# Self-loops under a sort key of their own, added as a scale per node, and hop loops of 102 written-out groups

## What is computed

```python
src = concatenate([s, d, arange(6250)]); dst = concatenate([d, s, arange(6250)])   # then sorted by dst

def spmm(edge_row, edge_col, edge_val, dense):
    msgs = edge_val[:, None] * dense[edge_col]
    return segment_sum(msgs, edge_row, num_segments=6250)

h = maximum(layernorm(x), 0)
support = h @ weight
h1 = spmm(src, dst, edge_weight, support)
h2 = spmm(src, dst, edge_weight, h1)
x = x + relu(hop_w[0] * h1 + hop_w[1] * h2 + h)
h = maximum(layernorm(x), 0)
agg = segment_sum(h[src], dst, num_segments=6250)
h = (1.0 + eps) * h + agg
h = elu(bn(h @ W1 + b1)); h = elu(bn(h @ W2 + b2)); h = elu(bn(h @ W3 + b3))
x = x + h @ W4 + b4
```

## Time and profile before

| what | us |
| --- | --- |
| median of 3 runs | 4452.27 (4449.58 to 4452.95) |
| the profiled execution | 4446.35 |
| its span, first to last instruction | 4444.7 |
| before hop 1's first gather | 452.3 |
| hop 1 | 1109.0 |
| hop 2 and the turn to the third gather | 1118.0 |
| third gather stage | 1060.7 |
| dense layers | 705 |

### The profile page before, as it was taken

The page is one execution under the profiler, slowest core; times in us unless marked ns, Lnnn a source line. Parts: engine busy times, 40 slices in busy tenths (PEclk is TensorE's granted clock), DMA queues, the critical chain, the costliest instruction groups (busy, mean ns, idle before and its releaser), DMA issues. The chain is left out here.

```text
span 4444.7 us, 50645 instructions
## 1 busy us (share of the span) xinstructions
PE 3284.7 (74%) x15959; PEld 2715.9 (61%) x15959; DVE 1873.4 (42%) x4492; ACT 797.2 (18%) x1969; POOL 2662.6 (60%) x2708
## 2 busy tenths in 40 slices
PE   6698677777777767777777774566666665998998
PEld 5297555555555555656555654555555555887887
DVE  7898333333333233333333332222222224556766
ACT  4098000000000000000000000000000001545656
POOL 1077677777777677777777766777777775001000
PEclk9899999999999999999999996788888887999999
DMA  4000333333333433333333344433333332223323
GB/s 142 1 5 13 96 108 113 110 109 109 114 109 108 101 104 109 109 114 109 109 108 112 109 99 134 125 105 105 104 105 104 105 105 87 98 89 134 95 65 116
DMA packets 205564, 443.83 MB, mean 100 GB/s; under 512 B 47053, under 2 KB 121089, under 8 KB 205289
## 3 DMA queue, kind: packets, MB, share of 16 engines
q0 software_dynamic: 126464, 336.63, 26.2%
q1 hardware_dynamic: 78933, 105.26, 7.2%
HBM read 382.22 MB, written 59.49 MB: 99 GB/s over the span
## 5 line engine op out<-in xcount | busy, mean ns | idle before, releaser
L1885 PE MATMUL ps<-work 128*128 128x256 f32 x6912 | 1615.3, 387 | 591.2 <-DMA work<-table_hop,idx 591.2
L792 POOL DMA_INDIRECT work<-table_hop,idx x1728 | 1660.2, 961 | 555.7 <-issue 522.1
L1885 PEld LDWEIGHTS ps<-work 128*128 128x128 f32 x6912 | 1288.5, 191 | 916.2 <-DMA work<-table_hop,idx 493.3
L837 POOL DMA_INDIRECT work<-table_gin,idx x832 | 791.0, 951 | 281.7 <-issue 229.5
L1960 PE MATMUL ps<-work 128*128 128x128 f32 x3328 | 571.8, 343 | 411.2 <-DMA work<-table_gin,idx 382.2
L1960 PEld LDWEIGHTS ps<-work 128*128 128x128 f32 x3328 | 526.1, 249 | 481.1 <-DMA work<-table_gin,idx 324.7
L1423 DVE TENSOR_SCALAR work<-iota,w_hi,edge_buf 128x256 f32<-128x256 bf16 x1728 | 583.4, 409 | 17.9 <-issue 16.6
L948 ACT COPY idx<-w 128x8 int32 (+1 forms) x216 | 42.3, 197 | 1951.7 <-PE ps L1885 1950.9
L1536 DVE TENSOR_TENSOR sum_b<-sum_b,ps 128x256 f32 x104 | 43.9, 422 | 799.2 <-PE ps L1960 799.2
L1435 DVE TENSOR_TENSOR sum_b<-sum_b,ps 128x512 f32 x108 | 74.2, 688 | 720.2 <-PE ps L1885 720.2
L1435 DVE TENSOR_TENSOR big<-big,ps 128x512 f32 x108 | 74.3, 688 | 694.2 <-PE ps L1885 694.2
(11 more groups left out here) (225 smaller groups left out, 2609.3 us busy)
## 6 DMA issues: line engine op xcount, KB each, us to landing
work<-table_hop,idx POOLq DMA_INDIRECT x1728, 2.7
z_dram<-sum_b SPq DMA_DIRECT2D x24, 964.0 KB, 4.1
sum_b<-z_dram SPq DMA_DIRECT2D x24, 964.0 KB, 5.2
work<-table_gin,idx POOLq DMA_INDIRECT x832, 2.7
big<-x SPq DMA_DIRECT2D x12, 512.0 KB, 6.0
table_hop<-work SPq DMA_DIRECT2D x12, 512.0 KB, 2.9
table_hop<-sum_b SPq DMA_DIRECT2D x12, 512.0 KB, 3.2
x_dram<-big SPq DMA_DIRECT2D x12, 512.0 KB, 3.5
```

Source lines behind the costliest of these rows:

```text
L792: pool.indirect_dma_start(hop_rows[:, par, t, :], None, table[n], bass.IndirectOffsetOnAxis(idx[:, k % HR, t:t + 1], 0)).then_inc(rows_in[ ...
L837: pool.indirect_dma_start(rows[:, par, t, :], None, table[2], bass.IndirectOffsetOnAxis(idx[:, q, t:t + 1], 0)).then_inc(rows_in[par][half ...
L1885: mm = pe.matmul(ps[:, HWIN * par + b, 0:D], hot[:, par, t, b * P:(b + 1) * P], hop_rows[:, par, t, :], start=(t == 0), stop=(t == GT - 1))
```

## The change

A loop gets the key 49, behind the windows (`NK` = 50 keys), so that the windows' edges fill 102 groups and the loops seven more behind them (`LGROUPS`), which no hop gathers. In the first eight groups of hop 1 DVE builds one-hots of the loops' nodes and PE sums the loop weight of each node with them (`loop_sum`). In hop 1 SP reads `support` back, chunk by chunk, and DVE adds it times `loop_sum` to the sums; hop 2's share of the loops is `loop_scale` on h1 in place of the constant of `keep_h1`. All 102 groups of both hops are written out. `make_bins` now works on bf16 pairs in two halves. Some semaphores are merged.

```diff
+NK = NT + 1
-HBODY = 18
-HITER = 6
-HGROUPS = HBODY * HITER
+HGROUPS = 102
+LGROUPS = 7
+TGROUPS = HGROUPS + LGROUPS
...
+PACE = 8.5
...
 def over_hop(eng, step):
 
-    for k in range(HBODY):
-        step(0, k, True, False)
-    with eng.Fori(1, HITER - 1) as i:
-        for k in range(HBODY):
-            step(i, k, False, False)
-    for k in range(HBODY):
-        step(HITER - 1, k, False, True)
+    for k in range(HGROUPS):
+        step(k)
...
+def chunk_at(k, at):
 
+    for c in range(FULL - 1):
+        if k == at + int(PACE * (c + 1)):
+            return c, c % 2
     return None, None
```

On SP's queue, in hop 1:

```diff
+            def support_load(c):
+                if c > 0:
+                    sp.wait_ge(loop_added, c)
+                sp.dma_start(support_in, rows_of(table[0], c, CT - 1)).then_inc(support_back, 16)
+                sp.dma_start(support_in3, table[0][c * CN + (CT - 1) * P:(c + 1) * CN, :]).then_inc(support_back, 16)
+
+            def hop1_step(k):
+                if k == GT:
+                    sp.wait_ge(loop_mm, GT)
+                    sp.dma_start(support_tail, table[0][FULL * CN:ROWS, :]).then_inc(support_back, 16)
+                    support_load(0)
+                c, q = chunk_at(k, 2)
                 if c is not None:
-                    sp.wait_ge(hop_add, HBODY * i + k + 1)
+                    support_load(c + 1)
+                    sp.wait_ge(hop_add, k + 1)
                     h1_out(c, CT)
```

On DVE, the keys and their one-hots at the start:

```diff
-            dve.wait_ge(edges_in, 64)
-            dve.tensor_copy(dst_all, dst_i).then_inc(dst_cast, 1)
+            dve.wait_ge(edges_in, 96)
+            dve.tensor_copy(dst_all, dst_i)
             dve.tensor_copy(src_all, src_i)
             chain(dve.tensor_scalar(ints, src_i, 7, 127, ALU.logical_shift_right, ALU.bitwise_and))
-            chain(dve.tensor_copy(bin_of, ints))
+            chain(dve.tensor_copy(packed, ints))
+            dve.tensor_tensor(ints.bitcast(F32), src_all, dst_all, ALU.is_equal).then_inc(dst_cast, 1)
+            dve.wait_ge(dst_cast, 1)
+            at_ = [P, TILES, 2]
+            chain(dve.scalar_tensor_tensor(out=bin_twice, in0=ints.bitcast(F32).unsqueeze(2).to_broadcast(at_), scalar=float(NT),
+                                           in1=packed.unsqueeze(2).to_broadcast(at_), op0=ALU.mult, op1=ALU.max))
...
             def make_bins(t):
 
-                windows = iota[:, 0:NT].unsqueeze(1).to_broadcast([P, BINS, NT])
-                of = bin_by_step[:, t, :].unsqueeze(2).to_broadcast([P, BINS, NT])
-                dve.tensor_tensor(bins_of_all(t), windows, of, ALU.is_equal).then_inc(bins_made, 1)
+                at_ = [P, HB, NK // 2, 2]
+                keys = iota[:, 0:NK].rearrange("p (a u) -> p a u", u=2).unsqueeze(1).to_broadcast(at_)
+                for half in range(2):
+                    of = bin_by_step[:, t, half * HB:(half + 1) * HB, :].unsqueeze(2).to_broadcast(at_)
+                    last = dve.tensor_tensor(bins_of(t, half).rearrange("p (g a u) -> p g a u", g=HB, u=2), keys, of, ALU.is_equal)
+                last.then_inc(bins_made, 1)
```

On DVE, in hop 1 (LSTEP is 7):

```diff
+            def loop_hots(k):
+                if k > 0:
+                    dve.wait_ge(loop_mm, k)
+                for u in range(LSTEP):
+                    n = LSTEP * k + u
+                    dve.tensor_scalar(loop_lo_hot[u], iota[:, 0:P], loop_lo[:, n:n + 1], w_sorted[:, HTILES + n:HTILES + n + 1],
+                                      ALU.is_equal, ALU.mult)
+                at_ = [P, LSTEP, NT]
+                dve.tensor_tensor(loop_hi_hot, iota[:, 0:NT].unsqueeze(1).to_broadcast(at_),
+                                  loop_hi[:, LSTEP * k:LSTEP * (k + 1)].unsqueeze(2).to_broadcast(at_),
+                                  ALU.is_equal).then_inc(loop_hot, 1)
...
+            def add_loops(c, tiles):
+                dve.wait_ge(support_back, 16 * (1 + 2 * min(c + 1, FULL)))
+                for t in range(tiles):
+                    of = support_tail if c == FULL else support_in3 if t == CT - 1 else support_in[:, t, :]
+                    b = CT * c + t
+                    to = hop1_sum[:, b * D:(b + 1) * D]
+                    last = dve.scalar_tensor_tensor(out=to, in0=of, scalar=loop_sum[:, b:b + 1], in1=to, op0=ALU.mult, op1=ALU.add)
+                last.then_inc(loop_added, 1)
...
+            def keep_h1_and_loops(c, tiles):
+                for t in range(tiles):
+                    b = CT * c + t
+                    to = base[:, b * D:(b + 1) * D]
+                    last = dve.scalar_tensor_tensor(out=to, in0=hop1_sum[:, b * D:(b + 1) * D], scalar=loop_scale[:, b:b + 1], in1=to,
+                                                    op0=ALU.mult, op1=ALU.add)
+                last.then_inc(h1_kept, 1)
...
+            def hop1_step(k):
+                group(0, k, hop1_sum)
+                if k < GT:
+                    loop_hots(k)
+                if k == GT:
+                    loop_scales()
+                c, q = chunk_at(k, 1)
                 if c is not None:
...
+                    add_loops(c, CT)
```

On PE, in hop 1:

```diff
+            def hop1_step(k):
+                hop_group(0, k)
+                if k < GT:
+                    pe.wait_ge(loop_hot, k + 1)
+                    for u in range(LSTEP):
+                        mm = pe.matmul(bank(4, NT), loop_lo_hot[u], loop_hi_hot[:, u, :], start=(k == 0 and u == 0),
+                                       stop=(k == GT - 1 and u == LSTEP - 1))
+                    mm.then_inc(loop_mm, 1)
```

More of the change, by code:

```diff
@@ L787, in gather @@
                 for half in range(2):
-                    if not (n == 0 and first and k < 2):
+                    if not (n == 0 and k < 2):
                         pool.wait_ge(hop_mm, 2 * (g - 2) + half + 1)
@@ L799, in _ @@
                 pool.wait_ge(sort_turned, 2)
-                over_hop(pool, lambda i, k, first, last: gather(0, i, k, first))
+                over_hop(pool, lambda k: gather(0, k))
                 pool.wait_ge(h1_stored, 16 * CHUNKS)
-                over_hop(pool, lambda i, k, first, last: gather(1, i, k, first))
+                over_hop(pool, lambda k: gather(1, k))
             with pool.Else():
@@ L955, in to_cols, with hop2_step @@
                                scale=eps_sb[:, 1:2]).then_inc(c_cols, 1)
-            def hop2_step(i, k, first, last):
-                fill_hop(1, i, k, first)
-                c, q = chunk_at(i, k, 5)
+            def hop2_step(k):
+                fill_hop(1, k)
+                c, q = chunk_at(k, 5)
                 if c is not None:
                     root(1, c, q, CT)
-                c, q = chunk_at(i, k, 7)
-                if first and c is not None:
+                c, q = chunk_at(k, 7)
+                if c == 0:
                     act.wait_ge(h1_kept, CHUNKS)
@@ L978, in _ @@
             with act.If(near):
-                over_hop(act, lambda i, k, first, last: fill_hop(0, i, k, first))
+                over_hop(act, lambda k: fill_hop(0, k))
                 over_hop(act, hop2_step)
@@ L1415, in far_hop, with build_hop @@
                     dve.wait_ge(far_done, 16 * n + 16)
[L1417 to L1419 removed]
+            def build_hop(n, k):
+                g = n * HGROUPS + k
+                if not (n == 0 and k < 2):
                     dve.wait_ge(hop_mm, 2 * (g - 1))
                 for t in range(GT):
[L1422 removed]
+                    at_ = bass.ds(k * GT + t, 1)
                     last = dve.tensor_scalar(hot[:, k % 2, t, :], iota[:, :], loc_sorted[:, at_], w_sorted[:, at_],
@@ L1435, in add_hop, with group @@
                 dve.tensor_tensor(to, to, ps[:, HWIN * par:HWIN * par + HWIN, 0:D], ALU.add).then_inc(hop_add, 1)
-            def group(n, i, k, first, last, sums):
-                if not (last and k == HBODY - 1):
-                    build_hop(n, i if k < HBODY - 1 else i + 1, (k + 1) % HBODY, first and k < HBODY - 1)
-                add_hop(n, i, k, first, sums)
+            def group(n, k, sums):
+                if k < HGROUPS - 1:
+                    build_hop(n, k + 1)
+                add_hop(n, k, sums)
@@ L1903, in _ @@
                 pe.wait_ge(sorted_ready, 1)
-                over_hop(pe, lambda i, k, first, last: hop_group(0, i, k, first))
+                over_hop(pe, hop1_step)
                 over_hop(pe, hop2_step)
```

288 lines of the change are left out of this document (160 added, 128 removed).

## The result

The changed kernel takes 4420.95 us (median of four runs, 4418.62 to 4422.07) where the kernel before takes 4451.7 in the same runs: a ratio of 0.993, 95% interval 0.991 to 0.995. It is faster by 31 us, not by the 111 that were forecast, and 4421 lies above the range (4324 to 4372). The profiled executions, 4446.35 and 4418.62 us, differ by 27.7.

The account below looks back on a forecast made before the run. POOL, issuing gathers end to end, was taken to bound the hops. Terms -121.0 + 5.7 + 1.5 + 1 + 2 = -110.8 us, from the median 4452.27, gave 4341 us; range 4324 to 4372.

Parts of the forecast that it names:

- Gathers removed: Both hops: 108 to 102 groups, 96 gathers fewer, 10.08 us saved per group, -121.0 us.
- Before the hops: Start to first gather: extra DVE compares, rank steps and tiny instructions, less time in `make_bins`; together +2 us.
- The loops' eight groups: First eight groups of hop 1: PE's step takes 11.1 us, 1.1 over POOL's pace, lag 9.5; +1 us.
- the 9.8 that PE may be late: In the hops: PE's half group could end 9.8 us later before the gather that waits for it starts.
- Holds in hop 2: Chunk ends of hop 2: gathers delayed by the 1,024-column DVE add rise from 5 to 11; +5.7 us.
- Holds in hop 1: Hop 1: gathers wait for one short DVE add at most, not whole blocks; with new compares, +1.5 us.
- SP's reads of support, scales, sums: Hop 1: 25 loads on SP's queue and DVE's extra adds fit into idle time; 0 us.
- Less gain: Rival: in hop 1, slow PE in loop groups and whole blocks of adds delay POOL; 4382 us, 11%.
- PE becomes the bound: Rival: in both hops PE's clock falls until PE, not POOL, sets the pace; 5284 us at 1.2 GHz, 2%.

Follow-up runs that it names:

- both faults mended: Changed kernel with its 109-row transfers issued as 108 rows and 1, and the loops' one-hots built ahead of DVE's add; 4343.7 us.
- early one-hots: Changed kernel with the loops' one-hots of a group built ahead of DVE's add of that group, same work; 4393.1 us.

## Why the prediction was wrong, step by step

- **Gathers removed, -121: right.** Six groups of hop 2 after, without a long add:

```profile
1705.20:1765.82 60.62, 45.99 (x48) 0.97 0.39 113
```

  10.10 us a group, in written-out code and with 102 groups. That POOL's gathers set a hop's length was right too.
- **Before the hops, +2: the step that failed, by 52 us.** It costed instructions of DVE, term by term, and their sum came out near: with the transfers mended the first gather is 3.5 us later. It put at nothing, without a reason, that the load of the list and the eight stores of zeros went from 108 to 109 rows. The sentence "The batches, the third gather and the dense layers are untouched" passed over the load between batches and hops, which is on the chain with nothing beside it. Measured, the load is 31.2 us longer and the scatters start 22.5 us later. No row before showed a transfer of a prime number of rows.
- **The loops' eight groups, +1: failed by 21 us, beyond its own upper bound of 17.** The mechanism was named and the order was read rightly, but the step of PE is 13.53, not 11.1 us. The lag is not "just under the 9.8 that PE may be late"; it uses that up by group 4. The 2.4 are the clock (8.82 for 7.41: 1.41), the products (1.60 for 0.85: 0.75) and the one-hots (0.27). The products were a misreading of the earlier trace rows: 202.1 us belong to 1,664 rows, but PE's queue has 832 of these matmuls, two rows for each, so seven cost 1.70 and not 0.85. Counted so, the prediction's own rows put PE 16.3 us late after eight groups, past the 9.8 by 6.5 (an estimate): the term would have been about +7 without any change of clock. The slow clock stood only in the upper bound, 2.1 us a group as after a long wait, although the change itself puts a wait of 3.1 us into each of the eight groups. A margin of 0.3 in 9.8 us could not carry the +1.
- **Holds in hop 2, +5.7: right.** Eleven of eleven, 1.83 to 1.96 us each, an excess of 10.4 in all for 4.8 before. One of them, to set beside the earlier trace rows:

```profile
1700.23 1.23 DVE L1535 SCALAR_TENSOR_TENSOR big<-big 128x1024 f32<-128x1024 f32 x1
1700.39 1.89 POOL L819 DMA_INDIRECT work<-table_hop,idx  x1 [0.30 <-issue]
```

- **Holds in hop 1, +1.5: mechanism right, the size off by 3.** POOL does get in between short adds. One of the eleven at the loops' adds:

```profile
1155.23 1.67 DVE L1515 SCALAR_TENSOR_TENSOR sum_b<-edge_buf,sum_b 128x256 f32<-128x256 f32 x4
1155.39 1.14 POOL L819 DMA_INDIRECT work<-table_hop,idx  x1 [0.30 <-issue]
```

  1.14 us, not 2.4 as for a whole block. The gathers that meet short adds lose 3.6 us in all, where 4.4 was forecast. All holds of hop 1 make 10.5 us for 5.9 all the same: the one-hot builds of the groups, for which the prediction has no term, now touch more gathers, about 0.1 us each. Hop 2 has the same, +2.7, and its last stretch, from the last gather's end to the next stage, lasted 26.7 for 24.1. Why, was not tested; over all profiles it is 25.7 to 27.7 with the change and 24.1 to 26.0 without.
- **SP's reads of support, scales, sums, 0: right**; early one-hots, with all of them in, have hop 1 at 1054.3.
- **The rivals.** "Less gain" had the right kind for the loops and missed the start. "PE becomes the bound" came true for six groups. None of them looked at a transfer.
- **The range.** It was said to follow from bounds of 4326 to 4360, but the bounds of the five terms add up to 4318 to 4388. The one of +26 for the holds in hop 1 does not take off the 4.0 that the holds before cost.

With both faults mended the kernel takes 4343.7 us where 4341 was forecast. That they lie so close is in part luck: between the two profiled executions the gain is 99.7 us (3.5 lost at the start, 55.7 and 50.0 gained in the hops, 2.5 lost behind them) where the sum has 110.8; the rest is that the profiled execution of the kernel before was faster than its median, and that of the mended kernel slower.

## What to carry to other kernels

When a shape goes up by one, count what it does to every DMA that has this shape, before counting instructions: look for a transfer alone on the chain and at its DMA share, and split off the rows that are over, or pad them. When a second engine's work is put between two steps of PE, price the step with the clock that PE will have after that wait, and build its operands a step ahead. A long two-input DVE instruction beside a stream of gathers is cheaper in pieces.

## What was not expected of the hardware

112 rows take no less time than 108, 5.4 against 5.0 us, although they can be cut into 16 equal shares and 108 into 12 at most: something else sets the time there, and no run here tells what. One engine moves 25 GB/s of these 8 KB rows, two 48. A slow store costs more than its own time: the eight stores of zeros hold SP, and all that stands behind them, for 32 us. And with a wait of 3.1 us ahead of the loop products PE began the next group near its lower clock in all eight groups behind such a wait: the granted clock over their first halves was 0.68 to 0.73.
